# A graph layer in one program: eleven Gram products and the zero stores moved behind the first barrier, the edge ids turned later, and a third routing buffer

## The reference, cut to what matters

```
xn = layernorm(x)
x  = x + gnn(xn, edges) + mix(xn)
x  = x + ffn(layernorm(x))
gnn: h = xn @ W (8 heads of 32); score = leaky(s_src[src] + s_dst[dst]);
     softmax over the edges of a node; out = sum of weight * h[src]
mix: attn = softmax(k^T v) per head (it needs only xn^T xn, the Gram matrix);
     x1 = xn + q attn; out = x1 + fc2(gelu(fc1(layernorm(x1))))
ffn: gate to 8 experts, the best two of each node, y = W2(gelu(W1 x)) weighted
```

## Time and profile before

| | us |
|---|---|
| median of three runs | 3615.82 |
| the profiled execution, its own time | 3604.1 |
| its span, first to last instruction | 3602.9 |
| node stage, to the first barrier | 0 to 235 |
| mix, and the first rows of the edges | 235 to 310 |
| edges | 310 to 2403 |
| merge | 2403 to 2495 |
| routing beside the experts | 2495 to 3210 |
| experts alone | 3210 to 3603 |

### The profile page before, as it was taken

One profiled execution on the slowest core, in us unless ns is written; L12 is line 12 of the kernel. 1 busy time (PEld: TensorE's weight loads), 2 busy tenths in 40 slices (PEclk: granted clock), 3 DMA queues, 4 the chain that ended last, 5 costly groups with the idle time before them and its releaser, 6 DMA issues.

```text
span 3602.9 us, 42119 instructions
## 1 busy us (share of the span) xinstructions
PE 2774.7 (77%) x11774; PEld 2174.0 (60%) x11774; DVE 2004.8 (56%) x5108; ACT 1423.8 (40%) x3176; POOL 2279.1 (63%) x2227
## 2 busy tenths in 40 slices
PE   6984888777887877787877777544287879899997
PEld 5863565555555655555655555432276768788886
DVE  5535666766665666666666766545445455542222
ACT  2322445444544544455444545330133333332232
POOL 0027777777777777777777777741546677764444
PEclk9987998989999989999998998875588889899999
DMA  8866565655556655565665665543467677787774
GB/s 197 273 203 167 162 163 161 180 160 161 164 159 164 180 164 159 161 164 159 168 174 161 164 163 151 153 114 114 148 170 213 176 209 202 187 205 164 162 156 86
DMA packets 433503, 607.21 MB, mean 169 GB/s; under 512 B 82736, under 2 KB 328444, under 8 KB 433197
## 3 DMA queue, kind: packets, MB, share of 16 engines
q0 software_dynamic: 126096, 302.66, 32.5%
q1 hardware_dynamic: 234239, 228.77, 21.7%
q10 hardware_dynamic: 72862, 72.45, 8.1%
HBM read 423.58 MB, written 181.80 MB: 168 GB/s over the span
## 4 chain that ended last, share of the span: by engine, by line
PE 48%; DVE 17%; DMA 12%; POOL 7%; issue 7%; ACT 6%; SPq 1%; ACTq 0%; POOLq 0%; DVEq 0%
PE bank L953 13%; PE bank L1760 7%; PE bank L808 6%; PE bank L1747 6%; DMA rows<-table,srcix 5%; PE bank L800 4%; DMA m_xs<-in_x 4%; POOL rows L890 3%; DVE rows L1086 3%; PE bank L520 2%; DMA e_fr<-frag,nodeix 1%; PE bank L1405 1%; POOL out L1828 1%; PE bank L512 1%; PE bank L513 1%
## 5 line engine op out<-in xcount | busy, mean ns | idle before, releaser
L890 POOL DMA_INDIRECT rows<-table,srcix x1664 | 1604.8, 964 | 506.9 <-issue 353.7
L953 PE MATMUL bank<-rows,onehot 128*128 128x272 f32 x3328 | 946.2, 435 | 28.9 <-ACT fout L1003 25.2
L1003 ACT ACTIVATE fout<-bank 128x272 f32<-128x272 f32 x1664 | 640.9, 398 | 487.8 <-PE bank L953 439.4
L953 PEld LDWEIGHTS bank<-rows,onehot 128*128 128x128 f32 x3328 | 683.9, 213 | 224.8 <-ACT fout L1003 44.3
L1086 DVE TENSOR_TENSOR rows<-rows,bank 128x1024 f32<-128x1024 f32 x416 | 482.8, 1213 | 167.0 <-ACT rows L994 167.0
L1828 POOL DMA_INDIRECT out<-x_y,x_dest x210 | 334.0, 1591 | 358.0 <-DMA out<-x_y,x_dest 206.1
L1760 PE MATMUL bank<-e_w,x_ht 128*128 x1680 | 406.4, 398 | 22.5 <-DVE x_y L1809 21.1
L1747 PE MATMUL bank<-x_int,x_w1c 128*128 128x256 f32 x1680 | 386.6, 384 | 3.6 <-issue 2.7
L1781 ACT ACTIVATE x_ht<-bank,x_b1c 128x256 f32<-128x256 f32 x420 | 173.9, 471 | 508.8 <-PE bank L1747 442.3
L1760 PEld LDWEIGHTS bank<-e_w,x_ht 128*128 128x128 f32 x1680 | 330.1, 202 | 69.5 <-issue 24.5
L1747 PEld LDWEIGHTS bank<-x_int,x_w1c 128*128 128x128 f32 x1680 | 322.8, 193 | 48.5 <-issue 3.0
(11 more groups left out here) (332 smaller groups left out, 3332.3 us busy)
## 6 DMA issues: line engine op xcount, KB each, us to landing
frag<-fout ACTq DMA_DIRECT2D x104, 544.0 KB, 4.5
x_w1c<-in_L_ffn_W SPq DMA_DIRECT2D x105, 512.0 KB
x_in<-sorted_d SPq DMA_DIRECT2D x105, 260.0 KB, 3.1
rows<-table,srcix POOLq DMA_INDIRECT x1664
x_b2c<-in_L_ffn_b SPq DMA_DIRECT2D x105, 128.0 KB, 3.6
frag<-zero SPq DMA_DIRECT2D x7, 1904.0 KB, 9.1
table<-hr SPq DMA_DIRECT2D x24, 544.0 KB, 4.5
xs<-in_x SPq DMA_DIRECT2D x24, 512.0 KB, 7.9
```

The costliest lines, as they stand in the source:

```text
L890: p.indirect_dma_start(out=B.rows[b][:, j, :], out_offset=None, in_=B.table[:, :], in_offset=bass.IndirectOffsetOnAxis(ap=B.srcix[:, col:c ...
L953: pe.matmul(B.banks[2 + c % 3][:, 0:ROW], B.onehot[k % 2][:, j, :], B.rows[k % NR][:, j, :], start=True, stop=True).then_inc(S.sum, 1)
L1003: a.activation(B.fout[k % 2][:, j, :], B.banks[2 + c % 3][:, 0:ROW], ACT.Copy).then_inc(S.ev, 1)
```

## The change

- The Gram products of the first 14 supers stay in the node stage, two behind every three supers; those of the last 11 move to the start of `mix_tensor`, behind the first barrier, with the copies of the Gram matrix. `xn` gets six buffers in place of three.
- The conversion of the edge ids stands behind the second pair on DVE, their transposes and copies behind super 3 on PE and ACT. The index steps start one pair later, and the histogram stands behind super 10 in place of 8.
- The zero stores go from SP's loop to the start of ACT's mix program, eight in a row; SP waits for them at the head of its edge program, ahead of the MLP's loads.
- Routing: `NF` is 3, `e_fr` and `e_x` are fetched two rounds ahead in place of one; ACT stores the sum and normalizes at step 26 of a round (before: stores at 4 and 8, normalizing from 22), and all later steps of a round stand 4 later.

The rest of the diff places buffers in memory and renames semaphores.

```diff
-NF, NH, W = 2, 3, 2 * ST
+NF, NH, W = 3, 3, 2 * ST
 
 AHEAD, NI, NW, NB = 3, 3, 4, 5
 NOUT = 6
-NXB = 3
+
+NXB, NXN, GRAM_LATE = 3, 6, 11
...
-    for b in range(NXB):
-        vec(v.memset(B.xn[b][:, :, D:D + 1], 1.0))
-    ids_vector(v, vec, S, B)
+    for x in B.xn:
+        vec(v.memset(x[:, :, D:D + 1], 1.0))
+    v.memset(B.zero[:, :], 0.0).then_inc(S.zero, 1)
     for q, pair in enumerate(X_PAIRS):
         b, n = q % NXB, sum(m for _, m in pair)
         v.wait_ge(S.a_x[b], sum(16 * len(X_PAIRS[i]) for i in range(b, q + 1, NXB)))
         v.wait_ge(vec.sem, vec.n)
         for _ in moments(v, vec, B.xs[b], B.st_a, n):
             pass
-        if q >= NXB:
-            v.wait_ge(S.gram, 2 * (q - NXB + 1))
-        normalize(v, vec, B.xs[b], B.xn[b], B.st_a, n, S.xn)
+        if q >= NXN:
+            v.wait_ge(S.gram, 2 * (q - NXN + 1))
+        normalize(v, vec, B.xs[b], B.xn[q % NXN], B.st_a, n, S.xn)
         if q == 0:
...
-            v.memset(B.zero[:, :], 0.0).then_inc(S.wcat, 1)
+        elif q == 1:
+            ids_vector(v, vec, S, B)
         else:
             next(index, None)
     for _ in index:
         pass
-    v.wait_ge(S.gram, NS)
-    for m in range(KD):
-        v.tensor_copy(B.gram[:, m, m * P:], B.banks[4 + m][:, m * P:D + 1]).then_inc(S.gcopy, 1)
-    v.wait_ge(S.gturn, 1)
-    vec(v.tensor_copy(B.gram[:, 1, 0:P], B.banks[4][:, 0:P]))
...
+ID_STEP = 3
+
+
+def gram(pe, S, B, k):
+    s, n = SUPERS[k]
+    xn, o = B.xn[k // 2 % NXN], k % 2 * ST
+    for i in range(n):
+        for m in range(KD):
+            t = pe.matmul(B.banks[4 + m][:, m * P:D + 1], xn[:, o + i, m * P:(m + 1) * P], xn[:, o + i, m * P:],
+                          start=(s + i == 0), stop=(s + i == TILES - 1))
+    t.then_inc(S.gram, 1)
...
+    grams = 0
     for k in range(NS):
         heads(k)
+        if k == ID_STEP:
+            pe.wait_ge(S.ix_fl, 6)
+            for i, (lo, n) in enumerate(TURNS):
+                if i >= 2:
+                    pe.wait_ge(S.ix_cp, i - 1)
+                for j in range(lo, lo + n):
+                    t = pe.transpose(B.banks[6 + i % 2][:, (j - lo) * P:(j - lo + 1) * P], B.ix_tmp[j // BLOCKS][:, j % BLOCKS, :], B.ident[:, :])
+                t.then_inc(S.ix_tp, 1)
         if k + 1 < NS:
             turn(k + 1)
-        gram(k)
-        if k == 8:
+
+        while grams < min((k + 1) * 2 // 3, NS - GRAM_LATE):
+            gram(pe, S, B, grams)
+            grams += 1
+        if k == 10:
...
+        if k == ID_STEP:
+            for i, (lo, n) in enumerate(TURNS):
...
-        if k % 3 == 1 and k // 3 < ZEROS:
-            lo = FAR + k // 3 * ZERO_TILES * P
-            sp.wait_ge(S.wcat, 5)
-            sp.dma_start(B.frag[lo:lo + ZERO_TILES * P, :].rearrange("(t p) d -> p t d", p=P),
-                         B.zero[:, :].unsqueeze(1).to_broadcast([P, ZERO_TILES, ROW])).then_inc(S.a_zero, 16)
-    sp.dma_start(B.frag[FRAGS - P:FRAGS, :], B.zero[:, :]).then_inc(S.a_zero, 16)
-    sp.wait_ge(S.a_zero, 16 * (ZEROS + 1))
...
+    for k in range(NS - GRAM_LATE, NS):
+        gram(pe, S, B, k)
+    pe.wait_ge(S.gcopy, 2)
+    pe.transpose(bk[4][:, 0:P], B.gram[:, 0, P:D], B.ident[:, :]).then_inc(S.gturn, 1)
...
+    v.wait_ge(S.gram, NS)
+    for m in range(KD):
+        v.tensor_copy(B.gram[:, m, m * P:], bk[4 + m][:, m * P:D + 1]).then_inc(S.gcopy, 1)
+    v.wait_ge(S.gturn, 1)
+    v.tensor_copy(B.gram[:, 1, 0:P], bk[4][:, 0:P]).then_inc(S.gcopy, 1)
...
+    a.wait_ge(S.zero, 1)
+    for i in range(ZEROS):
+        lo = FAR + i * ZERO_TILES * P
+        a.dma_start(B.frag[lo:lo + ZERO_TILES * P, :].rearrange("(t p) d -> p t d", p=P),
+                    B.zero[:, :].unsqueeze(1).to_broadcast([P, ZERO_TILES, ROW])).then_inc(S.a_zero, 16)
+    lo = FAR + ZEROS * ZERO_TILES * P
+    a.dma_start(B.frag[lo:FRAGS, :], B.zero[0:FRAGS - lo, :]).then_inc(S.a_zero, 16)
...
     beside = Beside(mlp_sync(sp, S, B))
+    sp.wait_ge(S.a_zero, 16 * (ZEROS + 1))
...
-TURN = MOMENTS + MOMENT_STEPS + LAG
+NORM = MOMENTS + MOMENT_STEPS + 4
+TURN = NORM + LAG
...
-                elif r and r + 1 < len(ROUNDS) and k < late + R_TILES[r + 1]:
-                    fetch(r + 1, k - late)
+                elif r >= 2 and r + 2 < len(ROUNDS) and k < late + R_TILES[r + 2]:
+                    fetch(r + 2, k - late)
...
+        if r in (1, 2):
+            for i in range(R_TILES[r + 1]):
+                fetch(r + 1, i)
...
-        if r + 1 < len(ROUNDS):
-            fetch(r + 1)
+        if r + 2 < len(ROUNDS):
+            fetch(r + 2)
...
+    fetch(1)
...
-        for i, k in enumerate(ROUNDS[r]):
+        yield from idle(NORM)
+
+        a.wait_ge(S.e_rx1, 2 * r + len(ROUNDS[r]))
+        a.wait_ge(S.e_mom, r + 1)
+        for k in ROUNDS[r]:
             s, m = SUPERS[k]
             o = s - R_FIRST[r]
-            yield from idle(4)
-            a.wait_ge(S.e_rx1, 2 * r + i + 1)
             full = min((N_NODES - s * P) // P, m)
             a.dma_start(rows_of(B.out, s, full), x[:, o:o + full, :]).then_inc(S.e_x1[r % NF], 16)
             if full < m:
                 a.dma_start(B.out[(s + full) * P:N_NODES], x[0:N_NODES - (s + full) * P, o + full, :]).then_inc(S.e_x1[r % NF], 16)
-        yield from idle(MOMENTS - 4 * len(ROUNDS[r]) + MOMENT_STEPS)
-
-        a.wait_ge(S.e_mom, r + 1)
```

More of the change, by code:

```diff
@@ L273, in __init__ @@
         mark_ix = nc.sbuf_base
+        self.rows = several("rows", NR, [P, CB, ROW])
+        mark_late = nc.sbuf_base
+        self.xn = several("xn", NXN, [P, 2 * ST, D + 1])
+        late_end = nc.sbuf_base
+        nc.sbuf_base = mark_late
+        self.onehot, self.fout = several("onehot", 2, [P, CB, P]), several("fout", 2, [P, CB, ROW])
+        mark_edges = max(nc.sbuf_base, late_end)
+        nc.sbuf_base = mark_ix
         self.di, self.si = A("dst_i", [P, BLOCKS, P], I32), A("src_i", [P, BLOCKS, P], I32)
+        self.ix_tmp = several("ix_tmp", 2, [P, BLOCKS, P])
@@ L573, in nodes_scalar @@
             a.activation(B.hr[b][:, i, :], B.banks[2 + (s + i) % 2][:, 0:ROW], ACT.Copy).then_inc(S.hr, 1)
+        if k == ID_STEP:
+            for i, (lo, n) in enumerate(TURNS):
+                bank = B.banks[6 + i % 2]
+                a.wait_ge(S.ix_tp, i + 1)
+                for j in range(lo, lo + n, n if (lo + n <= BLOCKS or lo >= BLOCKS) else 1):
+                    m = n if (lo + n <= BLOCKS or lo >= BLOCKS) else 1
+                    to = (B.loc, B.srcix)[j // BLOCKS]
+                    at = j % BLOCKS * P
+                    t = a.activation(to[:, at:at + m * P], bank[:, (j - lo) * P:(j - lo + m) * P], ACT.Copy)
+                t.then_inc(S.ix_cp, 1)
 def nodes_sync(sp, S, B):
@@ L646, in mix_tensor @@
     pe.wait_ge(S.mixv, 1)
+    pe.wait_ge(S.gcopy, 3)
     for m in range(KD):
```

54 lines of the change are left out of this document (13 added, 41 removed).

## The result

| | before | after |
|---|---|---|
| median of 4 runs, us | 3615.14 | 3563.27 |
| lowest and highest, us | 3611.26, 3618.37 | 3560.53, 3568.09 |
| profiled execution, us | 3604.1 | 3563.22 |

The ratio is 0.9858, with a 95% interval of 0.9841 to 0.9875: 52 us faster, where 59 had been forecast, inside the range of 3525 to 3592. This pair was measured on one chip. That is the larger part of what this study found. The pair was not run again, and the record does not name its chip: that the difference belongs to the chip, and not to the moment of measuring, is the likely reading and not a shown one.

A forecast was written before the change was run, and what follows sets the result against it. POOL was taken to bound the kernel behind the first barrier, nobody to be full in the routing rounds; 21 (node stage) - 2 (zero stores) + 40 (routing) = 59 us, median 3615.8 to 3557 us, range 3525 to 3592.

The forecast's parts named there:

- front of the node stage: Start of the node stage: ids turned later let super 4 start near 73 instead of 74; 1 us booked.
- nine Gram products: Node stage: nine supers lose a Gram product of 2.63 us, less 0.9 us waiting for ACT's copy; 16 us gained.
- the stall: Node stage, 146 us: PE's 6.96 us wait for `xn` and some 3 us of slow clock go; 5 us gained.
- mix: Behind the first barrier: eleven moved Gram products take 29 us on PE, but delay nothing POOL needs; cost 0.
- zero stores: Behind the first barrier: 13.3 MB of stores run beside POOL's gathers; 2 us lost, bounds 0 and 15.
- edges: From the first barrier on: POOL bounds the edges, so whatever is won ahead of the barrier is won in full.
- routing: Eight routing rounds: earlier gathers and four more steps cut PE's and POOL's waits; 40 us gained, bounds 15 and 60.
- The rival that hangs on it: Behind the first barrier: gathers share DMA three ways and the zeros cost 12 us; 3567 us, chance 0.09.
- the slower rival: Behind the first barrier: zeros hold the gathers, POOL stands still 78 us; 3633 us, chance 0.04.
- POOL is the bound: Routing rounds: scatter landings hold POOL, so perhaps 5 of 40 us come; gain 24, 3592 us, chance 0.14.
- its sign of being wrong: Routing rounds: POOL's waits for its own scatters grow by what its waits for DVE lose.
- two covers: Behind the first barrier: PE's existing wait for the weights, then 17 us between group 0's sums and POOL's need of its buffers.

The follow-up runs named there:

- grams_node: The change with all Gram products kept in the node stage, each behind the next super's turn; ratio 1.0002 to the kernel before on a slower chip.
- zeros_node: The change with the zero stores put back in SP's loop of the node stage; ratio 1.0051 to the kernel before on a slower chip.
- ids_front: The change with the edge ids converted and turned at the front again, as before; ratio 1.0126 to the kernel before on a slower chip.
- before_again: The kernel before, unchanged, run and profiled again on a slower chip; 4019.55 us, compared with itself 1.0017.
- node_only: The change with its routing part undone; ratio 1.0042 to the kernel before on a slower chip.
- node_only_b: The change with its routing part undone, run once more on another slower chip; 4035.6 us, ratio 1.0029 to the kernel before.
- route_only: The kernel before with the routing part of the change alone; 4023 us, ratio 1.0015 to the kernel before on a slower chip.
- after_again: The change itself, unaltered, run again on a slower chip; 4043.77 us, ratio 1.0040 to the kernel before.
- no_shift: The change without the four later routing steps, ACT storing out<-e_x during the moments wait as before; 4032.3 us, ratio 1.0009 to the kernel before.
- grams_no_shift: The change with all Gram products in the node stage and without the four later routing steps; ratio 1.0020 to the kernel before.
- mix_loads_first: The change with all Gram products in the node stage, no four later routing steps, mix-weight loads ahead of the ids' loads; ratio 0.9990 to the kernel before.

## Why the prediction was right

**The pair.** By its own terms, from the two profiles and the runs that isolate them:

| term | forecast | measured | read from |
|---|---|---|---|
| front of the node stage | 1 | 5.1 | super 4's heads at 68.9 for 74.0 |
| nine Gram products | 16 | 13.8 to 14.5 | 9 x 1.53; grams_node |
| the stall | 5 | 9 | grams_node against before |
| mix | 0 | 0 | 49th gather, no wait |
| zero stores | -2 | 0 | the same; zeros_node |
| edges | 0 | -12.5 | longer gathers on POOL, cause open |
| merge | 0 | -0.5 | its first gather |
| routing | 40 | 26.9 | 1107.3 to 1080.4 |
| sum of the profiles | 59 | 41.0 | spans |
| medians | 59 | 51.9 | |

*Front.* The forecast had super 0's heads at 22 us and super 3's at 59. They came at 29.1 (ACT was still issuing the ids' loads until 26.5, which the forecast overlooked) and 56.9. SP's late release (49.8; forecast 51) and the store of super 0 hold super 3 as said. The ids' transposes then take 4.3 us (62.7 to 67.0), not the 6 to 7 that were put down for them. These two, 2 us each, are the 4 us that the forecast was short.

*Gram products.* The mechanism and the size are right: PE waits 0.87 for ACT's copy, and 1.53 us are left of the 1.73 worked out.

*The stall.* It goes. The 5 us kept back for late loads were not needed: PE asks faster and x still comes in time. The forecast's reason, that the index steps stand one pair later, fits ids_front, where they stand a pair earlier and the stalls come back, 3.95 and 6.32 us; the conversion of the ids moved with them there, so the steps alone are not shown.

*Zero stores.* Free on both sides for POOL, which nothing covers. DMA queues of the changed kernel, 208 to 283 us (packets, MB, share of 16 engines; q10 is ACT's, q0 the gathers', q1 SP's):

```profile
q10 hardware_dynamic: 12746, 13.74, 53.2%
q0 software_dynamic: 2736, 7.94, 30.9%
q1 hardware_dynamic: 5285, 2.20, 10.5%
```

Three queues are loaded. POOL's 60 gathers took 57.01 us, as many as before in 56.92 (235 to 310 us), and followed each other at 1.25 us. By the Trainium skill's rule of turns between queues (DMA: Bandwidth & Descriptors, Queues, rings and completion order) the gathers were to fall to a third and, by the forecast's estimate, to 1.46 us. Their share did fall, from 38.9% to 30.9%, but they moved 7.94 MB for 8.19: it is the time of a packet that fell, from 166 to 135 ns in the mean, and POOL kept its pace. The rival that hangs on it gets nothing here, and the slower rival (the zeros hold the gathers) is refuted.

*Routing.* The step that was mis-sized. The waits fell by 42 us where 50 were forecast, DVE's for `e_fr` altogether, and eight rounds take 54.7 us each in place of 57.5 (53 against 57.9 in the forecast). Two things were missing from the sum. The first is the start: from the first gather of `e_fr` to the first result it takes 147.2 us, before 140.4. At the first scatter of the second round 6.5 us of that are there (87.2 for 80.7). ACT in the first round, timeline of the changed kernel, shows one part:

```profile
2505.54 0.96 ACTq L1463 DMA_DIRECT2D out<-e_x  x2
2506.55 4.04 ACT L1471 ACTIVATE e_hn<-e_x,e_st 128x256 f32<-128x256 f32 x8 [48.79 <-issue]
```

The two stores now stand between the moments (done at 2505.4) and `e_hn`, which starts 1.1 us later for them, in each of the two rounds that have no tiles to cover them. The larger part is PE's clock. The 32 gate products, in the profile of before and in that of the change:

```profile
2526.76 4.91 PE L1405 MATMUL bank<-e_gw,e_hnt 128*128 128x8 f32 x32 [0.73 <-issue]
```

```profile
2513.89 6.97 PE L1435 MATMUL bank<-e_gw,e_hnt 128*128 128x8 f32 x32 [0.73 <-issue]
```

The granted clock over these products is 0.73 in the first and 0.50, the lower of its two levels (1.2 GHz), in the second, and the second round shows the same (4.95 and 6.96 us): 4.1 us in both rounds together. This is not the change's: before_again, node_only and node_only_b, with the old routing, take 6.97 us too, and zeros_node and grams_node, with the new, 4.6 in the first round. The eight early gathers, which the forecast priced at up to 10 us, have no part in these 6.5 us, since they are issued behind that scatter, from 107.9 us on. On the other chips they have a price: PE waits for the rows of the second tile 10.6 to 11.7 us in five profiles with early gathers (route_only, after_again, no_shift, grams_no_shift, mix_loads_first) and 5.4 and 4.8 in before_again and node_only_b; in the pair it is 1.3 us with the change and 0.3 before.

The second is POOL. Of the 35.3 us that it no longer waits for DVE, 18.7 came back as waits for its own scatters. That is the rival "POOL is the bound", half true: I had allowed 5 us for it, and its sign of being wrong, that these waits grow by what those for DVE lose, came by half.

*The median.* The forecast took the profile's distance to the median, 11.7 us, as the same for both kernels; for the change it is 0.05, so the medians give 51.9 us and the profiles 41.0. What made the profiled execution of before quick is found only in part: the 4.1 us of the gate products, while its gathers were not quick. Against the 59 forecast, the profiles show the first barrier with the zero stores 8 us better, the routing 13 worse, and 12.5 us lost in the edges, which had no term. Errors of both signs stand against each other, and the differing distance to the median takes up 11 us of the rest. The mechanisms were right, but that 52 lies so near 59 is in part luck.

**The other chips.** The prediction gave the mix 0 because it had two covers, and said what would happen past them: POOL would wait for the sums of group 0. There it does, for 61 us, and 28 us of lead become a loss of 13. The mechanism is none of the rivals' and could not be read from the trace of before, in which PE is never held so. Its covers were counted in microseconds of one chip; the change put 168 products more into the stretch in which PE slows down. In after_again they take from 205.6 to 320.6 us, 115 in place of 29.5, and 24 of them start 2.8 us apart instead of 0.19.

## What to carry to other kernels

Work moved behind a barrier under the cover of a gather queue is only as cheap as the engine that does it stays fast beside that queue: count the moved instructions, not only their time, and look at a second chip before calling the cover safe. A busy DMA share is no price by itself; 13.3 MB of stores cost nothing at 0.82 and nothing at 0.95, because no wait ended on them. When a fetch is moved a round ahead, look for what the move puts behind it at the start, where no tile covers it, and for the next wait of the engine that ends the kernel.

## What the runs showed of the hardware that was not expected

This kernel took 3615 us on the pair's chip and 4019.6, 4025.3 and 4045.8 on three others, 11 to 12% more (with the reserve made at the result: the pair was not repeated). The edges make up 380 of the 421 us that lie between the profiles of before and before_again. DMA packets, POOL's gathers (0.95 us) and the whole node stage (first barrier at 235.1 and 234.6) take the same time on both kinds.

On the three slower chips PE starts its products mostly at multiples of 0.70 us, up to 2.80, from 14 to 20 us behind POOL's first gather (205.9 to 221, 224.1 to 238.6, 240.2 to about 260). In node_only POOL's last gather before its long wait is at 298.7 us; the starts of PE's products are 2.80 us apart up to 304.6, then 2.10 and 0.71, and from 310.9 on PE works without a gap, at 0.19 us a product (the last row ends with the view, at 320 us):

```profile
304.62 0.37 PE L495 MATMUL bank<-xn 128*128 128x129 f32 x1 [2.21 <-issue]
306.72 0.37 PE L495 MATMUL bank<-xn 128*128 128x129 f32 x1 [1.73 <-issue]
...
310.92 9.33 PE L495 MATMUL bank<-xn 128*128 128x257 f32 x48 [0.33 <-issue]
```

The granted clock is 0.53 from 221 to 300 us in after_again, close to the lower of its two levels (0.5, 1.2 GHz), but a product is busy there for 0.37 to 0.59 us, so the clock alone does not space them 2.80 apart. It is not DMA load either: with the engines fully busy and no gather PE kept 0.19 us. Nor does code loading show in that stretch: between 262 and 340 us node_only's trace has no 16 KB instruction packet and one of 8 KB, while PE's pace changes by a factor of 15. What on those chips links POOL's gathers to PE's pace stays open. In the edges it comes and goes: of the 119 us that PE stands in 310 to 1000 us, 29.6 are one wait in the mix and 89 are in the edges.
